# Ternary FFN weights in halves: four cuts and four signs spread over heads 4 to 10 of the first attention

## The chip, the cores and the metric

The kernel runs on one core of a Trainium2 chip. The metric is the device time of one launch in microseconds; lower is better. Each version is run several times and the median counts. A profiled execution also leaves a trace: the start and the duration of every instruction on TensorE (PE, with its weight loads as PEld), VectorE (DVE), ScalarE (ACT), GpSimd (POOL) and the queue engine SyncE (SP), and what ended each idle stretch.

## The reference

The input `x` is 16 samples of 256 tokens by 512. Each sample goes through an attention block that a condition vector modulates, and then through a feed-forward block with ternary weights; the result is added to `x`.

```python
# attention: 16 heads of 32
scale, shift = split(emb @ W_emb + b_emb)
xn = rms_norm(x, g_norm) * (1 + scale) + shift
q, k, v = heads(xn @ W_qkv)
q, k = rms_norm(q, g_q), rms_norm(k, g_k)
o = softmax(q @ k.T * 32 ** -0.5) @ v
y = o + o @ W_out
# feed-forward: 512 -> 2048 -> 512, both weights ternary
def ternarize_weights(w):
    gamma = mean(abs(w))
    return sign(round(w / (gamma + EPS))) * gamma
h = gelu(absmax_quant(layer_norm(y)) @ ternarize_weights(w_fc).T)
out = x + absmax_quant(layer_norm(h)) @ ternarize_weights(w_proj).T
```

Both ternary matrices have 512 x 2048 weights. They are made once, on the chip, while the first samples are already under way.

## The kernel before

The kernel is a pipeline by hand over the 16 samples. `iteration(i)` works on up to five samples at once: it stores sample i-2 (`late`), does the feed-forward block of i-1 (`ffn`), the attention of i (`att`), the q, k, v projections of i+1 (`qkv`) and the input statistics of i+2 (`pre`). Every engine has a program of its own in which these pieces stand in a fixed order; nothing is scheduled at run time. What one engine needs of another it waits for by a semaphore, and an instruction that waits holds back all that stands behind it on its engine.

This case plays in iteration 0, the first attention, which has no feed-forward part. Its loop over the 16 heads is the frame. For head h

- PE computes the scores into a bank of PSUM (L905, `SA` or `SB` by turns, once head 3 is past). It may do so when the bank's scores of two heads before have been read to the end (`plo_r`).
- ACT takes the exponential in place (L1252) and copies it to f16 (`p_hi`, L1258).
- DVE takes the rest, `p_lo` (L1608), which frees the bank.
- PE multiplies with the values, two heads later (`values`, L920 to L922). At the first head of a group of four these products need the shared bank `PV`, which DVE empties with L1457 and L1459 (`heads_out`: `rden`, `o_sb`).

Between the heads stands other work, put at a head by tables. PE computes the q and k of the next sample in four pieces of 512 columns; ACT squares a piece (L1272), DVE sums it (`ssq`, L1634), POOL raises the sums to the power -0.5 (`rqk`, L721), DVE scales the piece (`qkn`, L1638), PE turns it (L1101), ACT and DVE take it apart into f16 pairs (`qkT`, L1294, and L1654 or L1657). The outputs of a group of heads are turned too (L930) and split (`oT_hi` L1327, `oT_lo` L1465). All turns go through one bank `T`, which is free again when DVE has read it (`unturned`).

The ternary weights are made in the same loop. A matrix is held as four parts of 128 x 2048 f32. POOL scales and rounds a part by adding a large constant (L661 for `w_fc`, L691 for `w_proj`). Then the part becomes -1, 0 or 1 in f16, in one of two ways: DVE cuts it off with two instructions, `fc_cut` (L1368 and L1370), or ACT takes the sign with one, `signs` (L1159). `w_fc` parts 2 and 3 go by ACT ahead of the heads, parts 0 and 1 by DVE at heads 4 and 6 (`FC_CUT_AT`). Of `w_proj` ACT does parts 0 and 1 at heads 5 and 6 (`SIGN_AT`), and parts 2 and 3 behind the last head. A sign of `w_proj` writes where a raw part of `w_fc` has lain, so it waits for the cut of that part (`s_fcut`). Who reads the ternary weights comes in iteration 1: `column_sums` on PE (sums of `w_proj`, L767) and `up` (L1005).

Of the kernel before, what the change touches and what calls it, by code (L numbers as in the profile page):

```python
# [16 lines left out]
F = 4 * D  # L17
# [24 lines left out]

HALVES = slice(0, D // 2), slice(D // 2, D)
PIECES = [(0, 0), (0, 1), (1, 0), (1, 1)]

# [56 lines left out]
POOL_PROJ_ROUNDS = (0, 1), (2, 3)  # L102
FC_CUT_AT = {4: 0, 6: 1}
SIGN_AT = {5: (1, 0), 6: (1, 1)}
SIGNS = [(0, 2), (0, 3)] + [SIGN_AT[h] for h in sorted(SIGN_AT)] + [(1, 2), (1, 3)]
WQ_LOW_UNIT, WQ_LOW_AT = {0: (0, 0, KT), 2: (1, 0, KT // 2)}, {1: (1, KT // 2, KT), 2: (2, 0, KT)}
WQ_LOW_DONE = (1, 3, 4)
COLSUM_PART = (0, 1), (1, 2), (2, 4)


# [119 lines left out]
def adaln_ffn_kernel(nc, x, xT, condT, w_emb, b_emb, g_norm, g_qk, w_qkv, w_out, w_fcT, w_projT, out):  # L230
    with ExitStack() as ctx:  # L231
# [274 lines left out]
        def ternary_rows(w, k):  # L506

            return fc_t[:, k, :] if w == 0 else proj_t[:, 4 * k:4 * k + 4, :].rearrange("p k n -> p (k n)")
# [224 lines left out]
        def _(pe):  # L733
# [29 lines left out]
            def column_sums(c):  # L763

                pe.wait_ge(s_sign, SIGNS.index((1, c)) + 1)
                for k in range(4 * c, 4 * c + 4):
                    mm = pe.matmul(FB[0][:, :], ones16[:, :], proj_t[:, k, :], start=(k == 0), stop=(k == FT - 1))  # L767
                if c == 3:
                    mm.then_inc(s_cs, 1)
# [49 lines left out]
            def iteration(i):  # L819
# [221 lines left out]
                for n in range(UNITS):  # L1041
                    if ffn is not None:
                        if n == 0 and not last(ffn):
                            pe.wait_ge(unturned, turn(i, ("y", 1)) + 1)
                        if first(ffn) and n == 0:
                            pe.wait_ge(s_fcut, 2)
                            pe.wait_ge(s_sign, 2)
# [88 lines left out]
        def _(act):  # L1136
# [13 lines left out]

            def signs(w, k):

# [4 lines left out]
                if w:  # L1157
                    act.wait_ge(s_fcut, k // 2 + 1)
                act.activation(ternary_rows(w, k), ffn_raw[w][k], ACT.Sign, bias=unmagic[:, 0:1]).then_inc(s_sign, 1)  # L1159

# [173 lines left out]
        def _(dve):  # L1334
# [26 lines left out]

            def fc_cut(k):

                dst = ternary_rows(0, k)
                if k == 0:
                    dve.wait_ge(wo_h, 2)
                dve.wait_ge(fc_round, POOL_ROUNDS.index(k) + 1)
                dve.tensor_scalar(dst, ffn_raw[0][k], MAGIC, 1.0, ALU.subtract, ALU.min).then_inc(s_cut, 1)  # L1368
                dve.wait_ge(s_cut, k + 1)
                dve.tensor_scalar(dst, dst, -1.0, None, ALU.max).then_inc(s_fcut, 1)  # L1370
# [161 lines left out]
            def iteration(i):  # L1532
# [67 lines left out]
                for h in range(HEADS):  # L1600
# [93 lines left out]
                    if isinstance(i, int) and i == 0 and h in FC_CUT_AT:  # L1694
                        fc_cut(FC_CUT_AT[h])
                    if h == OUT1_AT and ffn is not None:
# [48 lines left out]
```

## Time and profile before

| | us |
|---|---|
| median of 3 runs | 1085.83 |
| lowest, highest | 1084.81, 1086.24 |
| the profiled execution: its time | 1087.22 |
| the same: span from first to last instruction | 1085.2 |
| the same: what lies around the span | 2.0 |
| PE busy, DVE busy, ACT busy, POOL busy | 1051.3, 914.3, 800.6, 559.0 |
| heads of iteration 0, about | 57 to 97 |

The table says which engine has the most to do over the whole span; it does not say what a stretch of 40 us inside it waits for. For that the trace is read by its timeline: each row gives the start, the duration, the engine and the line, and in brackets how long the engine had been idle and which instruction released it.

### The profile page before, as it was taken

What the parts mean: (1) busy time and instruction counts of PE and PEld (TensorE: products, weight loads), DVE (VectorE), ACT (ScalarE), POOL (GpSimd) and SP (SyncE); (2) the same over time, 40 slices, a digit from 0 to 9 for tenths busy, and PEclk for the clock granted to TensorE, in tenths of its full rate; (3) what the DMA queues carried; (4) which work ended last, traced back from release to release, by engine and by line L of the source; (5) the groups of instructions that cost most, each with busy time, mean ns of one, the idle gap of its engine ahead of it and who ended that gap; (6) DMA issues with size and microseconds to landing.
All of it is one profiled execution on the core that took longest, in us unless ns stands there. A gap on an engine that the chain in (4) does not pass through costs nothing. (4 is left out here: it accounts for less than half of the span.)

```text
span 1085.2 us, 24403 instructions
## 1 busy us (share of the span) xinstructions
PE 1051.3 (97%) x9457; PEld 666.1 (61%) x9457; DVE 914.3 (84%) x1629; ACT 800.6 (74%) x1367; POOL 559.0 (52%) x372
## 2 busy tenths in 40 slices
PE   8679999999999999999999999999999999999898
PEld 2334766666576665656666665666656566665666
DVE  4888889888898888989898898989889898868767
ACT  4887877868687785868768586876858688584854
POOL 1953653809356290835629184471917447192613
PEclk9889999999999999999999999999999999999999
DMA  9923112131321313131131312204132220212100
GB/s 343 333 53 73 51 31 74 40 86 58 79 64 23 78 43 79 64 66 61 34 83 45 79 64 55 70 26 93 45 79 65 50 64 32 59 40 60 59 20 21
DMA packets 79698, 77.13 MB, mean 71 GB/s; under 512 B 8656, under 2 KB 60256, under 8 KB 79072
## 3 DMA queue, kind: packets, MB, share of 16 engines
q1 hardware_dynamic: 79552, 75.58, 25.6%
q8 instruction: 75, 1.23, 0.5%
q14 instruction: 39, 0.32, 0.1%
q10 hardware_dynamic: 32, 0.01, 0.0%
HBM read 41.85 MB, written 8.40 MB: 46 GB/s over the span
## 5 line engine op out<-in xcount | busy, mean ns | idle before, releaser
L1005 PE MATMUL F<-yT_hi,fc_t 128*128 128x256 f16 (+1 forms) x1024 | 224.9, 272 | 0.0
L1006 PE MATMUL F<-yT_lo,fc_t 128*128 128x256 f16 (+1 forms) x1024 | 224.6, 272 | 0.0
L721 POOL TENSOR_TENSOR rqk<-ssq,half 128x16 f32<-128x16 f32 x64 | 195.8, 3067 | 36.3 <-DVE ssq L1634 36.3
L843 PE MATMUL F<-proj_t,hs 128*128 128x512 f16 (+1 forms) x512 | 191.7, 376 | 0.0
L845 PE MATMUL F<-proj_t,hs 128*128 128x512 f16 (+1 forms) x512 | 191.3, 375 | 0.0
L1442 DVE SCALAR_TENSOR_TENSOR hs<-hg,g_inv,hs 128x512 f16<-128x512 f32 x128 | 147.7, 1164 | 27.5 <-ACT hs L1309 27.4
L679 POOL TENSOR_TENSOR acc<-acc,hg 128x512 f32<-128x512 f32 x96 | 146.9, 1530 | 14.3 <-ACT hg L1237 1.1
L686 POOL TENSOR_TENSOR acc<-acc,hq 128x512 f32<-128x512 f32 x90 | 114.2, 1269 | 14.2 <-DVE hq L1438 6.0
L1237 ACT ACTIVATE hg<-F,g_fc 128x512 f32<-128x512 f32 x128 | 87.2, 682 | 39.2 <-PE F L1006 38.8
L669 POOL TENSOR_TENSOR rs<-var,half 128x1 f32<-128x1 f32 x32 | 17.7, 552 | 183.8 <-DVE var L1428 183.8
L920 PEld LDWEIGHTS PV<-v_hi,p_hi 128*128 128x128 f16 x1024 | 88.1, 96 | 37.3 <-issue 10.9
L1005 PEld LDWEIGHTS F<-yT_hi,fc_t 128*128 128x128 f16 x1024 | 100.1, 98 | 17.7 <-issue 6.3
L673 POOL TENSOR_TENSOR rx<-msx,half 128x2 f32<-128x2 f32 x16 | 12.4, 776 | 188.9 <-DVE msx L1340 188.9
L920 PE MATMUL PV<-v_hi,p_hi 128*128 128x33 f16 x1024 | 104.5, 178 | 3.6 <-DVE o_sb L1459 2.2
L1006 PEld LDWEIGHTS F<-yT_lo,fc_t 128*128 128x128 f16 x1024 | 100.2, 98 | 11.1
L922 PE MATMUL PV<-v_hi,p_lo 128*128 128x33 f16 x1024 | 103.6, 177 | 0.0
L921 PE MATMUL PV<-v_lo,p_hi 128*128 128x32 f16 x1024 | 103.4, 177 | 0.0
L1608 DVE TENSOR_TENSOR p_lo<-SA,p_hi 128x512 f16<-128x512 f32 x123 | 84.5, 687 | 22.2 <-ACT p_hi L1258 22.1
L921 PEld LDWEIGHTS PV<-v_lo,p_hi 128*128 128x128 f16 x1024 | 83.5, 96 | 23.6 <-issue 0.3
L1608 DVE TENSOR_TENSOR p_lo<-SB,p_hi 128x512 f16<-128x512 f32 x123 | 84.4, 686 | 14.9 <-ACT p_hi L1258 12.1
L1309 ACT ACTIVATE hs<-hg,g_inv 128x512 f16<-128x512 f32 x128 | 92.4, 722 | 5.1
L1252 ACT ACTIVATE SA<-SA 128x512 f32<-128x512 f32 x123 | 72.2, 587 | 14.5 <-PE SA L905 13.7
(265 smaller groups left out, 2756.1 us busy)
## 6 DMA issues: line engine op xcount, KB each, us to landing
stk<-qkT SPq DMA_DIRECT2D x128, 128.0 KB, 2.5
xtok<-in_x SPq DMA_DIRECT2D x17, 512.0 KB, 3.9
xT_sb<-in_xT SPq DMA_DIRECT2D x16, 512.0 KB, 3.5
stk<-qkT SPq DMA_DIRECT2D x128, 64.0 KB, 2.2
xres<-in_x SPq DMA_DIRECT2D x15, 512.0 KB, 3.6
out<-xres SPq DMA_DIRECT2D x15, 512.0 KB, 2.8
stk<-in_w_emb SPq DMA_DIRECT2D x4, 512.0 KB, 6.7
fc_t<-in_w_qkv SPq DMA_DIRECT2D x2, 1024.0 KB, 11.1
```

What stands on the lines that cost most here:

```text
L679: pool.tensor_tensor(acc[:, 0, :], hg[:, 0, :] if n == 1 else acc[:, 0, :], hg[:, n, :], ALU.add).then_inc(sumh_r, 1)
L686: pool.tensor_tensor(acc[:, 1, :], hq[:, 0, :] if n == 1 else acc[:, 1, :], hq[:, n, :], ALU.add).then_inc(sumq_r, 1)
L721: pool.tensor_tensor(rqk[:, n % 2, :], ssq[:, n % 2, :], half[:, :], ALU.pow).then_inc(rqk_r, 1)
L843: pe.matmul(dst, hs[:, 0, k // 2, col:col + P], proj_t[:, k, cols], start=(k == 0), stop=False)
L845: mm = pe.matmul(dst, hs[:, 1, k // 2, col:col + P], proj_t[:, k, cols], start=False, stop=(k == FT - 1))
L920: pe.matmul(dst, ph, v_hi[:, k, h, :], start=(k == 0), stop=False)
L921: pe.matmul(dst[:, 0:DH], ph, v_lo[:, k, h, :], start=False, stop=False)
L922: mm = pe.matmul(dst, p_lo[:, h % (BEHIND + 1), k, t * P:(t + 1) * P], v_hi[:, k, h, :], start=False, stop=(k == TT - 1))
L1005: pe.matmul(dst, w, yT_hi[:, k, cols], start=(k == 0), stop=False)
L1006: mm = pe.matmul(dst, w, yT_lo[:, k, cols], start=False, stop=(k == KT - 1))
L1442: dve.scalar_tensor_tensor(hs[:, 1, n, :], hg[:, n, :], g_inv[:, 0:1], hs[:, 0, n, :], ALU.mult, ALU.subtract).then_inc(hlo_r, 1)
L1608: dve.tensor_tensor(p_lo[:, h % (BEHIND + 1), :, :], score_bank(att, h)[:, :].rearrange("p (k n) -> p k n", k=TT), p_hi[:, h % (BEHIND + 1 ...
```

## The change

The four jobs of the heads loop are cut in half by columns, and the tables place eight halves where four wholes were. `fc_cut(k, part)` does 1024 of the 2048 columns with its two instructions, at heads 4 and 5 (part 0 of `w_fc`), 6 and 8 (part 1). `signs(w, k, part)` does 1024 columns, at heads 6 and 7 (`w_proj` part 0), 9 and 10 (part 1). The semaphores count the halves: a sign of `w_proj` parts 0 and 1 waits for two halves cut, parts 2 and 3 and `up` for four. `signed(w, k)` gives the count of signs after which part k is complete. Nothing of what is computed changes, and PE's and POOL's orders stay as they were.

```diff
+F_HALVES = slice(0, F // 2), slice(F // 2, F)
...
-FC_CUT_AT = {4: 0, 6: 1}
-SIGN_AT = {5: (1, 0), 6: (1, 1)}
+FC_CUT_AT = {4: (0, 0), 5: (0, 1), 6: (1, 0), 8: (1, 1)}
+SIGN_AT = {6: (1, 0, 0), 7: (1, 0, 1), 9: (1, 1, 0), 10: (1, 1, 1)}
...
+def signed(w, k):
+    return max(n for n, sign in enumerate(SIGNS) if sign[:2] == (w, k)) + 1
...
-                pe.wait_ge(s_sign, SIGNS.index((1, c)) + 1)
+                pe.wait_ge(s_sign, signed(1, c))
...
-                            pe.wait_ge(s_fcut, 2)
+                            pe.wait_ge(s_fcut, 4)
...
-            def signs(w, k):
+            def signs(w, k, part=None):
+                cols = slice(0, F) if part is None else F_HALVES[part]
...
-                    act.wait_ge(s_fcut, k // 2 + 1)
-                act.activation(ternary_rows(w, k), ffn_raw[w][k], ACT.Sign, bias=unmagic[:, 0:1]).then_inc(s_sign, 1)
+                    act.wait_ge(s_fcut, 2 * (k // 2 + 1))
+                act.activation(ternary_rows(w, k)[:, cols], ffn_raw[w][k][:, cols], ACT.Sign, bias=unmagic[:, 0:1]).then_inc(s_sign, 1)
...
-            def fc_cut(k):
+            def fc_cut(k, part):
-                dst = ternary_rows(0, k)
-                if k == 0:
+                dst = ternary_rows(0, k)[:, F_HALVES[part]]
+                if k == 0 and part == 0:
                     dve.wait_ge(wo_h, 2)
                 dve.wait_ge(fc_round, POOL_ROUNDS.index(k) + 1)
-                dve.tensor_scalar(dst, ffn_raw[0][k], MAGIC, 1.0, ALU.subtract, ALU.min).then_inc(s_cut, 1)
-                dve.wait_ge(s_cut, k + 1)
+                dve.tensor_scalar(dst, ffn_raw[0][k][:, F_HALVES[part]], MAGIC, 1.0, ALU.subtract, ALU.min).then_inc(s_cut, 1)
+                dve.wait_ge(s_cut, 2 * k + part + 1)
                 dve.tensor_scalar(dst, dst, -1.0, None, ALU.max).then_inc(s_fcut, 1)
```

The first place is DVE at heads 4 to 6. `fc_t<-proj_t` and `fc_t<-fc_t` are the two instructions of a cut, `rden` and `o_sb` empty `PV` for the second group of heads, `p_lo` is the rest of heads 4 (`SA`), 5 (`SB`) and 6 (`SA`). Before:

```order
L1608 TENSOR_TENSOR p_lo<-SA,p_hi 128x512
L1368 TENSOR_SCALAR fc_t<-proj_t 128x2048
L1370 TENSOR_SCALAR fc_t<-fc_t 128x2048
L1457 RECIPROCAL rden<-PV 128x8
L1459 TENSOR_TENSOR o_sb<-PV,rden 128x256
L1608 TENSOR_TENSOR p_lo<-SB,p_hi 128x512
L1634 TENSOR_REDUCE ssq<-sq 128x16
L1638 TENSOR_TENSOR qkn<-QA,rqk 128x512
L1608 TENSOR_TENSOR p_lo<-SA,p_hi 128x512
L1465 TENSOR_TENSOR oT_lo<-T,oT_hi 128x256
L1368 TENSOR_SCALAR fc_t<-proj_t 128x2048
L1370 TENSOR_SCALAR fc_t<-fc_t 128x2048
```

And in the changed kernel, whose lines are numbered seven higher there:

```order
L1615 TENSOR_TENSOR p_lo<-SA,p_hi 128x512
L1375 TENSOR_SCALAR fc_t<-proj_t 128x1024
L1377 TENSOR_SCALAR fc_t<-fc_t 128x1024
L1464 RECIPROCAL rden<-PV 128x8
L1466 TENSOR_TENSOR o_sb<-PV,rden 128x256
L1615 TENSOR_TENSOR p_lo<-SB,p_hi 128x512
L1641 TENSOR_REDUCE ssq<-sq 128x16
L1645 TENSOR_TENSOR qkn<-QA,rqk 128x512
L1375 TENSOR_SCALAR fc_t<-proj_t 128x1024
L1377 TENSOR_SCALAR fc_t<-fc_t 128x1024
L1615 TENSOR_TENSOR p_lo<-SA,p_hi 128x512
L1472 TENSOR_TENSOR oT_lo<-T,oT_hi 128x256
```

The first cut has half the columns, and its second half stands behind `qkn` and ahead of `p_lo` of head 6.

The second place is ACT at heads 5 to 8. `proj_t<-hq` is a sign; `sq<-QB` closes head 5. Before:

```order
L1272 ACTIVATE sq<-QB 128x16x32
L1159 ACTIVATE proj_t<-hq,unmagic 128x2048
L1252 ACTIVATE SA<-SA 128x512
L1258 ACTIVATE p_hi<-SA 128x512
L1327 ACTIVATE oT_hi<-T 128x256
L1159 ACTIVATE proj_t<-hq,unmagic 128x2048
L1252 ACTIVATE SB<-SB 128x512
L1258 ACTIVATE p_hi<-SB 128x512
L1294 ACTIVATE qkT<-T 128x4x128
L1252 ACTIVATE SA<-SA 128x512
L1258 ACTIVATE p_hi<-SA 128x512
```

And in the changed kernel:

```order
L1279 ACTIVATE sq<-QB 128x16x32
L1259 ACTIVATE SA<-SA 128x512
L1265 ACTIVATE p_hi<-SA 128x512
L1334 ACTIVATE oT_hi<-T 128x256
L1166 ACTIVATE proj_t<-hq,unmagic 128x1024
L1259 ACTIVATE SB<-SB 128x512
L1265 ACTIVATE p_hi<-SB 128x512
L1301 ACTIVATE qkT<-T 128x4x128
L1166 ACTIVATE proj_t<-hq,unmagic 128x1024
L1259 ACTIVATE SA<-SA 128x512
L1265 ACTIVATE p_hi<-SA 128x512
```

The sign ahead of head 6 is gone; a half stands behind `oT_hi` of head 6 and another behind `qkT` of head 7.

The third place is ACT at heads 9 to 11. Before:

```order
L1252 ACTIVATE SB<-SB 128x512
L1258 ACTIVATE p_hi<-SB 128x512
L1294 ACTIVATE qkT<-T,g_k 128x4x128
L1252 ACTIVATE SA<-SA 128x512
L1258 ACTIVATE p_hi<-SA 128x512
L1327 ACTIVATE oT_hi<-T 128x256
L1252 ACTIVATE SB<-SB 128x512
```

And in the changed kernel:

```order
L1259 ACTIVATE SB<-SB 128x512
L1265 ACTIVATE p_hi<-SB 128x512
L1301 ACTIVATE qkT<-T,g_k 128x4x128
L1166 ACTIVATE proj_t<-hq,unmagic 128x1024
L1259 ACTIVATE SA<-SA 128x512
L1265 ACTIVATE p_hi<-SA 128x512
L1334 ACTIVATE oT_hi<-T 128x256
L1166 ACTIVATE proj_t<-hq,unmagic 128x1024
L1259 ACTIVATE SB<-SB 128x512
```

Two halves are new here, ahead of the exponentials of heads 10 and 11. On DVE the fourth half of the cuts comes behind the third `ssq`, at head 8.

## Rows read from the trace of the kernel before

**Rows 1.** The page: busy time, share of the span and instructions of each engine.

```profile
PE 1051.3 (97%) x9457; PEld 666.1 (61%) x9457; DVE 914.3 (84%) x1629; ACT 800.6 (74%) x1367; POOL 559.0 (52%) x372
```

**Rows 2.** Windows: stretch and its length, busy time by engine, granted PE clock, DMA.

```profile
57.00:76.50 19.50, 13.01 (x139) 7.27 (x137) 16.78 (x30) 17.06 (x30) 11.36 (x5) 1.00 0.25 62
76.50:83.30 6.80, 6.28 (x30) 3.14 (x31) 5.00 (x10) 4.42 (x9) 2.90 (x1) 0.50 0.01 2
83.30:98.00 14.70, 13.39 (x157) 8.27 (x154) 12.13 (x26) 10.44 (x20) 6.98 (x3) 1.00 0.07 15
200.00:300.00 100.00, 99.95 (x928) 61.97 (x926) 86.48 (x164) 72.86 (x133) 49.63 (x34) 1.00 0.25 60
```

**Rows 3.** Timeline of PE, heads 6 to 12: start, duration, instruction, idle time before.

```profile
70.35 0.18 PE L920 MATMUL PV<-v_hi,p_hi 128*128 128x33 f16 x1 [1.52 <-DVE o_sb L1459]
...
74.19 0.63 PE L1101 MATMUL T<-ident,qkn 128*128 128x128 f32 x4 [1.31 <-DVE oT_lo L1465]
...
77.03 0.61 PE L905 MATMUL SB<-stk 97*128 97x256 f16 x2 [1.69 <-DVE p_lo L1608]
...
80.55 1.09 PE L1101 MATMUL T<-ident,qkn 128*128 128x128 f32 x4
...
86.13 0.39 PE L773 MATMUL QA<-wq_hi,xn_hi 128*128 128x512 f16 x1 [0.79 <-DVE qkn L1638]
```

**Rows 4.** Timeline of DVE, heads 4 to 7.

```profile
67.01 1.90 DVE L1368 TENSOR_SCALAR fc_t<-proj_t 128x2048 f16<-128x2048 f32 x1
68.94 0.69 DVE L1370 TENSOR_SCALAR fc_t<-fc_t 128x2048 f16<-128x2048 f16 x1
...
70.12 0.68 DVE L1608 TENSOR_TENSOR p_lo<-SB,p_hi 128x512 f16<-128x512 f32 x1
...
72.43 0.69 DVE L1638 TENSOR_TENSOR qkn<-QA,rqk 128x512 f32<-128x512 f32 x1 [1.01 <-POOL rqk L721]
73.03 0.68 DVE L1608 TENSOR_TENSOR p_lo<-SA,p_hi 128x512 f16<-128x512 f32 x1
...
73.96 1.22 DVE L1368 TENSOR_SCALAR fc_t<-proj_t 128x2048 f16<-128x2048 f32 x1
...
76.28 0.69 DVE L1608 TENSOR_TENSOR p_lo<-SB,p_hi 128x512 f16<-128x512 f32 x1 [0.37 <-ACT p_hi L1258]
```

**Rows 5.** Timeline of POOL, 39 to 91 us; a row with x2 merges two instructions.

```profile
39.34 0.69 POOL L673 TENSOR_TENSOR rx<-msx,half 128x2 f32<-128x2 f32 x1
...
63.90 3.93 POOL L691 TENSOR_SCALAR hq<-hq,inv 128x2048 f32<-128x2048 f32 x2 [8.65 <-DVE wo_lo L1379]
67.79 1.88 POOL L673 TENSOR_TENSOR rx<-msx,half 128x2 f32<-128x2 f32 x1
69.46 5.80 POOL L721 TENSOR_TENSOR rqk<-ssq,half 128x16 f32<-128x16 f32 x2
...
87.61 3.07 POOL L721 TENSOR_TENSOR rqk<-ssq,half 128x16 f32<-128x16 f32 x1 [5.26 <-DVE ssq L1634]
```

**Rows 6.** Timeline of ACT, heads 5 to 12.

```profile
67.28 0.59 ACT L1272 ACTIVATE sq<-QB 128x512 f32<-128x512 f32 x1
69.73 2.00 ACT L1159 ACTIVATE proj_t<-hq,unmagic 128x2048 f16<-128x2048 f32 x1 [1.86 <-DVE fc_t L1370]
71.64 0.58 ACT L1252 ACTIVATE SA<-SA 128x512 f32<-128x512 f32 x1
72.31 0.60 ACT L1258 ACTIVATE p_hi<-SA 128x512 f16<-128x512 f32 x1
...
81.68 0.69 ACT L1294 ACTIVATE qkT<-T,g_k 128x512 f16<-128x512 f32 x1 [2.10 <-PE T L1101]
...
84.64 0.38 ACT L1327 ACTIVATE oT_hi<-T 128x256 f16<-128x256 f32 x1 [1.09 <-PE T L930]
84.92 0.59 ACT L1252 ACTIVATE SB<-SB 128x512 f32<-128x512 f32 x1
...
88.42 0.60 ACT L1294 ACTIVATE qkT<-T 128x512 f16<-128x512 f32 x1 [0.55 <-PE T L1101]
```

More of the change, by code:

```diff
@@ L1694, in iteration @@
                     if isinstance(i, int) and i == 0 and h in FC_CUT_AT:
-                        fc_cut(FC_CUT_AT[h])
+                        fc_cut(*FC_CUT_AT[h])
                     if h == OUT1_AT and ffn is not None:
```

## Prediction

> **What bounds the kernel now.** I read the busy line first [rows 1]: PE is busy 97% of the span. Then I compared stretches [rows 2]: from 200 to 300 us PE is busy 99.95 of 100 us, so there only PE's own work counts and anything gained or lost earlier is carried to the end unchanged. From 57 to 76.5 us, where the change lies, PE is busy only 13.01 of 19.50 us, and no engine is full (DVE 16.78, ACT 17.06). This stretch is bound by waits between in-order engines. From 76.5 to 83.3 us PE's granted clock is 0.50, the lower level of 1.2 GHz, and before and behind it 1.00.
>
> Third, the timeline of PE for what ended its waits. Three stand before the clock falls [rows 3]: 1.52 us for `o_sb`, 1.31 us for `oT_lo`, 1.69 us for `p_lo` of head 7. Each is followed back in the other timelines:
> - `o_sb` stands behind the first cut on DVE, which starts at 67.01 and ends at 69.63 (68.94 + 0.69) [rows 4].
> - `oT_lo` stands behind `p_lo` of head 6, and that behind `qkn`, which waited 1.01 us for POOL's power until 72.43 [rows 4].
> - `p_lo` of head 7 waited for ACT, where two signs of 2.00 us stand around head 6, the first after 1.86 us of waiting for the cut [rows 4, 6].
>
> So the whole-sized jobs do lie on the path. The question is where the halves come to lie.
>
> **What a half costs.** `L1368` took 1.22 us at 73.96 and 1.90 at 67.01 [rows 4]. The longer one began while POOL's L691 ran, which ended at 67.83 (63.90 + 3.93) [rows 5]; I read the 0.68 us between as DVE waiting for POOL. A half should then cost 0.61 us and the second instruction 0.35 (half of 0.69), 0.95 for a pair against 1.90 without the wait. Per-instruction overhead is not halved, so the truth is at or slightly above this; a half can't cost more than the whole. The sign: half of 2.00 plus a little, 1.05 us, with 0.1 of it beside its neighbour, as 69.73 + 2.00 overlaps 71.64 [rows 6]. Work added by the splitting: two DVE pairs and two ACT instructions more, by overhead alone some 0.1 us each.
>
> **Part by part, head by head.**
> 1. First half cut, head 4. It ends at 67.01 + 0.68 + 0.95 = 68.65 instead of 69.63, a gain of 0.9 to 1.0. If the 0.68 halves as well, the gain is 1.3; if nothing but the elements counts less, 0.8. I take 0.9, nearest the clean 1.22 row. `o_sb`, `p_lo` of head 5, PE's products at 70.35 and its scores of head 7 come 0.9 earlier.
> 2. The sign ahead of head 6 is gone. ACT is free after `sq` at 67.87 [rows 6], so the exponential of head 6 starts at about 67.8 instead of 71.64. This looks like 3.8 us, but it is spent at once: what reads it, `p_lo` of head 6, stands on DVE behind `qkn` and now behind a half cut.
> 3. POOL's `rx` took 1.88 us, 0.69 when alone, and ended with DVE's cut (67.79 + 1.88 = 69.67) [rows 5]. The power for `qkn` follows it. With the cut over 0.9 earlier, the power ends at 71.5, `qkn` starts at 71.5 instead of 72.43, the half cut takes 72.1 to 73.05, and `p_lo` of head 6 starts at 73.05: before 73.03 [rows 4]. The gain is exactly eaten. Bounds: if POOL doesn't start earlier, it is 0.9 later; if the cut costs less, 0.1 earlier. `oT_lo`, and PE's turn at 74.19 behind it, stay where they were.
> 4. ACT's first half sign waits for that second half cut: 73.15 to 74.2. Then the exponential and copy of head 7 (steps of 0.68 and 0.60, as in rows 6) end at 75.4, and `p_lo` of head 7 starts at 75.5 instead of 76.28, after the third half cut, which fits ahead of it from 74.0 to 74.95. PE's scores of head 9 start at 76.25 instead of 77.03: a gain of 0.8.
> 5. The second half sign, behind `qkT` at 75.35 to 75.9, ends at 76.9; the exponential of head 8 starts at 76.8, before 76.6 (0.2 later).
> 6. PE's pieces and the turn at 80.55 come 0.75 earlier, 79.8, since PE is at half clock in both. ACT's `qkT` comes at 80.95 instead of 81.68. Before, ACT had idled 2.10 us there [rows 6], but now the third half sign follows, 81.5 to 82.5, and the exponential of head 10 starts at 82.5 instead of 82.3.
> 7. PE reaches the turn for `oT_hi` 0.4 earlier (the clock comes back at 83.3 in either kernel, so work done before that point is worth half): `oT_hi` 84.25 instead of 84.64. The fourth half sign stands behind it, 84.5 to 85.5, so the exponential of head 11 starts at 85.45 instead of 84.92: 0.5 later.
> 8. What is late next: ACT idled 0.55 us before `qkT` at 88.42 [rows 6] and takes up that 0.5. PE's wait of 0.79 at 86.13 for `qkn` ends up to 0.4 earlier. The `ssq` that starts POOL's last power, 87.61 + 3.07 = 90.68 [rows 5], comes 0.5 later, and its reader began at 90.8; so 0.4 late there, mostly behind PE work, since PE is busy 13.39 of 14.70 us in that stretch [rows 2]. I keep 0 to +0.25.
>
> Sum: -0.9 at head 6, 0 at head 6's rest, -0.8 at head 9, +0.5 at head 11, absorbed at head 12: between -0.4 and +0.3 at the end of the heads, and I take -0.1. Behind it are four half waits that don't bind: `column_sums` and `up` need the halves at 101 us and later, all are done by 86. The profiled execution would go from 1087.22 (span 1085.2 + 2.0) to 1087.1; its time lies 1.4 above the median shown, and applied to the median 1085.83 the forecast is 1085.7.
>
> **The rivals.**
> *A, the clock stays up.* The fall at 76.5 follows a stretch in which PE waited 1.31 and 1.69 us with little between [rows 3]. Of this the second wait shrinks to 0.9, but the first grows: PE arrives 0.9 earlier at a turn that stays at 74.19, so 2.2 us. The total is the same 3.1, so I expect the fall to come again. For the rival: it lies otherwise in time, and after 75.5 PE is better fed. If it doesn't fall, the turn comes at 78.5 instead of 79.8, DVE's `o_sb` and ACT's half signs decide, and the exponential of head 11 starts at 83.8 instead of 84.92: -1.1, time 1084.7.
>
> *B, the second half cut is late.* If POOL's power isn't moved by the shorter cut, `qkn` stays at 72.43 and the half cut pushes `p_lo` of head 6 and the first half sign 0.9 back. Then every step from 3 on is 0.9 later; the idle of ACT before its turns (2.10, 1.09, 0.55) takes up part of it. Price +0.3 to +0.9, time 1086.4. It decides as soon as the power ends later than 71.5. For it: one POOL row only shows the coupling. Against it: that `rx` ended within 0.05 us of the cut.
>
> *C, a cut is shut out by POOL's power.* The second half cut starts at 72.1, when POOL works on its second power, 71.5 to 74.4 (2.90 each, rows 5). If DVE had to wait for the power's end, the pair would end at 75.3, `p_lo` of head 6 start 2.2 later and PE's turn with it; after the idle of ACT is used up, +1.6 remain, time 1087.4, slower than before. It decides from 71.5 on, whenever a power runs at the cut's start. Against it stands the cut at 73.96: the power ran until 75.26 (69.46 + 5.80), and `L1368` took its plain 1.22 us [rows 4, 5].
>
> The Trainium skill, "SBUF — State Buffer", section on what the engines share, makes rival C a rule: a VectorE `tensor_scalar` in a two-port mode and a GpSimd instruction exclude each other for the whole instruction, and the later one fully blocks. By that rule the sum would be 1087.4. The trace agrees for L691 against L1368 (0.68 us lost) and for `rx` (1.88 against 0.69), and disagrees for the power; the measurement decides, so C gets a small chance.
>
> **How the numbers follow.** My forecast has 0.56, A 0.24, B 0.13, C 0.04; 0.03 is for what I haven't seen. What a measurement of this kernel can tell from no change is 0.2%, 2.2 us. The forecast and B lie well inside it, A reaches it only with another microsecond from the scatter of the runs (1084.81 to 1086.24), C for about one case in three. So faster 0.05, same 0.91, slower 0.04. The range runs from A with 0.5 us of scatter below, 1084.2, to B's far end, 1086.7, with 0.3 above: 1087.0.
>
> **What would show it.** Right: the half `L1368` at head 4 at about 1.3 us and the others at 0.6; `p_lo` of head 6 within 0.2 of where it was relative to the scores of head 4; ACT waiting over 2 us for the second half cut; the exponential of head 9 earlier and that of head 11 later. A: a clock row without 0.50 between 70 and 85. B: `qkn` at 72.4. C: an `L1368` of 128x1024 that takes over 1.5 us beside a power. The forecast is wrong if the first matmul of iteration 1's `up` moves by more than 1 us.

## The result, and the profile after

The changed kernel is slower: median 1087.88 us (1086.51 to 1089.57, 22 runs) against 1086.16 us (1084.58 to 1088.20, 22 runs) of the kernel before on the same chip, a ratio of 1.0016 with a 95% interval of 1.0010 to 1.0022. Forecast were 1085.7 us, a range of 1084.2 to 1087.0, and no change, with 0.91. The ratio lies inside the 0.2% that the prediction took for its limit of no change, but its interval leaves out 1.0000, and the median lies above the range; 0.33 us of the distance is the kernel before, whose median had been 1085.83 in the 3 runs shown ahead. The profiled execution took 1088.09 us, with a span of 1086.2 us. In two of the experiments below one run took 3.7 ms, and the ratios leave it out.

The busy line of the page of the changed kernel (engine, busy us, share, instructions) answers to [rows 1]:

```profile
PE 1053.2 (97%) x9457; PEld 665.6 (61%) x9457; DVE 915.1 (84%) x1633; ACT 800.5 (74%) x1369; POOL 559.0 (51%) x372
```

Four instructions more on DVE and two on ACT cost 0.8 us and nothing in busy time. PE's busy time rose by 1.9 us at the same 9457 instructions; the same instruction lasts longer at the lower clock (the scores of head 9 below 0.61 us, 0.39 at the full clock). So no engine has gained work that would account for the loss; where the time goes has to be read stretch by stretch. The windows of the changed kernel, with the columns of [rows 2]:

```profile
57.00:76.50 19.50, 14.42 (x141) 7.80 (x139) 16.29 (x32) 14.57 (x29) 11.29 (x5) 0.93 0.26 62
76.50:83.30 6.80, 6.02 (x45) 3.08 (x46) 5.92 (x12) 6.03 (x10) 3.04 (x1) 0.75 0.01 2
83.30:98.00 14.70, 12.51 (x141) 7.76 (x141) 11.98 (x26) 11.65 (x22) 7.22 (x4) 1.00 0.07 14
200.00:300.00 100.00, 99.93 (x921) 61.95 (x920) 86.64 (x164) 72.74 (x131) 50.14 (x34) 1.00 0.25 60
```

The second row reads 0.75 where [rows 2] have 0.50: this execution had 3.4 us of the lower clock in the heads, and the profiled one of before had 6.8 (added up over windows of 1 us). The 0.93 of the first row is the end of an earlier stretch of low clock, which lasted until 56.0 us in the trace of before and until 59.8 here. It cost nothing in the heads: the exponential of head 5 comes 7.53 to 7.55 us after that of head 0 in every trace of this document, in one of which that stretch lasted until 63.2 (signs alone, filled). ACT now has 2.5 us less work ahead of 76.5 (14.57 against 17.06) and 1.6 more from 76.5 to 83.3: the signs have moved there.

DVE at heads 4 to 8 of the changed kernel answers to [rows 4]:

```profile
67.14 1.35 DVE L1375 TENSOR_SCALAR fc_t<-proj_t 128x1024 f16<-128x1024 f32 x1
68.53 0.43 DVE L1377 TENSOR_SCALAR fc_t<-fc_t 128x1024 f16<-128x1024 f16 x1
...
69.44 0.68 DVE L1615 TENSOR_TENSOR p_lo<-SB,p_hi 128x512 f16<-128x512 f32 x1
...
71.98 0.69 DVE L1645 TENSOR_TENSOR qkn<-QA,rqk 128x512 f32<-128x512 f32 x1 [1.25 <-POOL rqk L727]
72.59 0.68 DVE L1375 TENSOR_SCALAR fc_t<-proj_t 128x1024 f16<-128x1024 f32 x1
73.31 0.43 DVE L1377 TENSOR_SCALAR fc_t<-fc_t 128x1024 f16<-128x1024 f16 x1
73.65 0.68 DVE L1615 TENSOR_TENSOR p_lo<-SA,p_hi 128x512 f16<-128x512 f32 x1
...
78.89 0.69 DVE L1615 TENSOR_TENSOR p_lo<-SA,p_hi 128x512 f16<-128x512 f32 x1 [0.81 <-ACT p_hi L1265]
```

PE and POOL there, to [rows 3] and [rows 5]:

```profile
74.81 0.63 PE L1107 MATMUL T<-ident,qkn 128*128 128x128 f32 x4 [2.61 <-DVE oT_lo L1472]
...
76.93 0.61 PE L911 MATMUL SB<-stk 97*128 97x256 f16 x2 [0.98 <-DVE p_lo L1615]
```

```profile
67.91 1.16 POOL L679 TENSOR_TENSOR rx<-msx,half 128x2 f32<-128x2 f32 x1
69.05 6.27 POOL L727 TENSOR_TENSOR rqk<-ssq,half 128x16 f32<-128x16 f32 x2
80.27 3.28 POOL L727 TENSOR_TENSOR rqk<-ssq,half 128x16 f32<-128x16 f32 x1 [4.95 <-DVE ssq L1641]
```

And ACT at heads 6 to 11, to [rows 6]:

```profile
67.89 0.60 ACT L1259 ACTIVATE SA<-SA 128x512 f32<-128x512 f32 x1
...
73.83 1.15 ACT L1166 ACTIVATE proj_t<-hq,unmagic 128x1024 f16<-128x1024 f32 x1 [3.02 <-DVE fc_t L1377]
74.89 0.57 ACT L1259 ACTIVATE SB<-SB 128x512 f32<-128x512 f32 x1
...
81.69 1.14 ACT L1166 ACTIVATE proj_t<-hq,unmagic 128x1024 f16<-128x1024 f32 x1
82.73 0.59 ACT L1259 ACTIVATE SA<-SA 128x512 f32<-128x512 f32 x1
...
84.17 1.15 ACT L1166 ACTIVATE proj_t<-hq,unmagic 128x1024 f16<-128x1024 f32 x1
85.21 0.60 ACT L1259 ACTIVATE SB<-SB 128x512 f32<-128x512 f32 x1
```

The last two half signs start with no idle time ahead of them and hold up the exponentials of heads 10 and 11 by 1.04 us each (81.69 to 82.73, 84.17 to 85.21). Before, ACT had idled 2.10 and 1.09 us there ahead of `qkT` and `oT_hi` [rows 6].

**How the two profiled executions differ.** I cut both at three points: the exponential of head 0, the first `bn` of iteration 1 (end of the heads), and DVE's write of `mrow` in iteration 1, from where PE is full.

| stretch, us | before | changed | difference |
|---|---|---|---|
| start to exponential of head 0 | 58.56 | 58.69 | +0.13 |
| to the first `bn` of iteration 1 | 41.39 | 41.34 | -0.05 |
| to `mrow` of iteration 1 | 21.65 | 21.64 | -0.01 |
| to the end | 963.61 | 964.50 | +0.89 |

At first sight the heads are innocent. That reading is false, since the two had unlike clocks, and the 0.89 is a second matter.

### The profile page after: what moved, and what is told of

It is laid out like the page before. It is cut to its first block and busy times, and to the rows that moved or that the text cites. A ratio compares the mean times of both kernels' runs of the same rounds, so it can differ in the third digit from the quotient of the medians.

```text
span 1086.2 us, 24411 instructions
## 1 busy us (share of the span) xinstructions
PE 1053.2 (97%) x9457; PEld 665.6 (61%) x9457; DVE 915.1 (84%) x1633; ACT 800.5 (74%) x1369; POOL 559.0 (51%) x372
```

## The experiments

Each kernel ran 11 times, the kernel before beside it 27 or 33 times on the same chip (medians 1086.03 to 1086.31), and a ratio compares these two. "Heads", "low clock" and "rest" are those of the one profiled execution. "Heads" is the second row of the table above, "rest" the last; "low clock" is how long TensorE was granted 1.2 GHz in the heads from 66 us on. The expectations below take the end of a trace to 0.1 us, so their rests are up to 0.05 us off (963.96 for 964.01 or 963.92).

| kernel | median | ratio to before, 95% | heads | low clock | rest |
|---|---|---|---|---|---|
| before again | 1086.40 | 1.0002 (0.9993 to 1.0011) | 41.32 | 6.8 | 963.56 |
| changed again | 1087.42 | 1.0011 (1.0003 to 1.0020) | 41.82 | 6.8 | 963.92 |
| before, filled | 1084.64 | 0.9985 (0.9977 to 0.9994) | 39.01 | 0 | 963.55 |
| changed, filled | 1087.97 | 1.0014 (1.0005 to 1.0023) | 41.10 | 0 | 964.34 |
| cuts alone | 1087.63 | 1.0014 (1.0005 to 1.0023) | 41.42 | 6.8 | 963.86 |
| signs alone | 1086.44 | 1.0004 (0.9995 to 1.0013) | 41.35 | 3.4 | 963.51 |
| cuts alone, filled | 1086.77 | 1.0008 (0.9999 to 1.0017) | 42.03 | 3.4 | 963.89 |
| signs alone, filled | 1085.24 | 0.9995 (0.9986 to 1.0004) | 39.81 | 0 | 963.55 |
| split in place | 1087.05 | 1.0013 (1.0004 to 1.0021) | 41.14 | 6.8 | 963.93 |
| before, four memsets | 1086.61 | 1.0001 (0.9992 to 1.0010) | 40.28 | 3.4 | 963.95 |
| gap | 1085.86 | 0.9998 (0.9989 to 1.0007) | 39.55 | 3.4 | 963.95 |
| gap, filled | 1084.65 | 0.9988 (0.9979 to 0.9997) | 38.24 | 0 | 964.01 |
| single wait | 1087.53 | 1.0012 (1.0003 to 1.0021) | 41.08 | 3.4 | 963.99 |
| changed, twelve memsets | 1087.71 | 1.0014 (1.0005 to 1.0023) | 41.70 | 6.8 | 963.71 |
| gap, filled, twelve memsets | 1084.52 | 0.9984 (0.9975 to 0.9992) | 38.25 | 0 | 963.88 |

**The two kernels again.** No edit.

> The kernel before, unchanged, as a control: ratio 1.000. It also gives a second trace and the granted clock of each run. Clock theory (the change makes TensorE's clock fall in the first attention more often, or for longer, than before): most of its runs spend less time at the lower clock than the trace shown before, whose stretch at 0.50 lasted 6.8 us, and have a higher mean clock than those of the changed kernel. Order theory (the half signs ahead of the exponentials of heads 10 and 11 hold ACT back, whatever the clock does): no difference in mean clock. Landing theory (loads land by chance, the two medians differ by which loads PE meets): the point at which iteration 1 starts is the same in both kernels and the difference arises behind 108 us.

> The changed kernel, unchanged: ratio 1.001 to 1.002 as measured. Clock theory: lower mean clock than before_again by the stretch that it loses, some 3 us at half clock (0.0015 of the mean). Order theory: same mean clock, first up-projection matmul about 1.5 us later than in before_again. Landing theory: first up-projection matmul at the same time as in before_again, within 0.3 us.

The loss is there again, somewhat smaller. This trace of the changed kernel had 6.8 us of low clock as that of before has, and its heads are 0.46 us longer (41.82 against 41.36, the mean of 41.39 and 41.32). So some loss is there at an equal clock. The clock theory isn't ruled out beside it: the granted clock of whole runs is 0.9910 on average in these 11 and 0.9902 in the 22 of the result, against 0.9919 in the 11 of before again and 0.9909 to 0.9916 in the runs of before beside the experiments. A difference of 0.001 is some 2.2 us more at half clock, and a mean doesn't say whether they lie in the heads or ahead of them, where they cost nothing.

**Filling TensorE's waits.** Small products on a free bank (`keep_busy`) stand in the waits of heads 6 to 9, so that the clock stays up. The edit is the same in all filled kernels, with other counts:

```diff
+BUSY_SCORES, BUSY_VALUES, BUSY_TURN = {9: 4}, {6: 2}, {7: 10}
...
+                                keep_busy(FB[0], BUSY_SCORES.get(h, 0))
```

> The changed kernel with dummy matmuls of TensorE into a free bank in its three waits: 2 ahead of the values of head 4, 10 ahead of the turn at head 7, 4 ahead of the scores of head 9 (0.22 us each, so they fit into waits of 0.7, 2.6 and 1.0 us). Clock theory: the clock stays up, and the kernel gains 1 to 2 us, ratio 0.999 to 1.000. Order theory: ACT and DVE decide, so it stays at 1.0016. Landing theory: it stays at 1.0016.

> The kernel before with dummy matmuls of TensorE into a free bank in its three waits: 5 ahead of the values of head 4, 5 ahead of the turn at head 7, 6 ahead of the scores of head 9 (waits of 1.5, 1.3 and 1.7 us). Clock theory: if before rarely falls, no gain, ratio 1.000; if it falls as in its trace, up to 1.5 us faster, ratio 0.9985. Order theory and landing theory: at most 0.5 us faster.

The kernel before gains 0.15% from a clock that stays up, the changed one gains nothing. Exponential of head 11, counted from that of head 0: 26.36 to 23.70 us in the kernel before, 26.52 to only 26.29 in the changed one. The small products themselves hold nothing up: the exponential of head 9 comes at 20.53 in the changed kernel and 19.72 in that before, within 0.02 of where it came without them. ACT of the filled kernel before, heads 9 to 11:

```profile
80.16 0.69 ACT L1300 ACTIVATE qkT<-T,g_k 128x512 f16<-128x512 f32 x1 [0.33 <-PE T L1107]
80.75 0.59 ACT L1258 ACTIVATE SA<-SA 128x512 f32<-128x512 f32 x1
...
82.23 0.38 ACT L1333 ACTIVATE oT_hi<-T 128x256 f16<-128x256 f32 x1 [0.21 <-PE T L931]
82.51 0.59 ACT L1258 ACTIVATE SB<-SB 128x512 f32<-128x512 f32 x1
```

And the same stretch of the filled changed kernel:

```profile
81.13 0.68 ACT L1307 ACTIVATE qkT<-T,g_k 128x512 f16<-128x512 f32 x1
81.70 1.15 ACT L1172 ACTIVATE proj_t<-hq,unmagic 128x1024 f16<-128x1024 f32 x1
82.74 0.60 ACT L1265 ACTIVATE SA<-SA 128x512 f32<-128x512 f32 x1
...
84.38 0.38 ACT L1340 ACTIVATE oT_hi<-T 128x256 f16<-128x256 f32 x1 [0.36 <-PE T L937]
84.66 1.14 ACT L1172 ACTIVATE proj_t<-hq,unmagic 128x1024 f16<-128x1024 f32 x1
85.70 0.59 ACT L1265 ACTIVATE SB<-SB 128x512 f32<-128x512 f32 x1
```

With a fast TensorE, ACT's idle of 2.10 us [rows 6] has shrunk to 0.33 in the first listing: there is no room for a half sign any more. In the second, two of them stand in ACT's nearly full row (0.36 us idle). So at an equal clock the change costs in the heads: 0.46 us with 6.8 us of low clock, 1.06 with 3.4 (41.34 against 40.28, the kernel before with four memsets, below), 2.09 with none (41.10 against 39.01).

**Half of the change at a time.** Cuts alone keeps the whole signs at heads 5 and 6, signs alone the whole cuts at 4 and 6:

```diff
-SIGN_AT = {6: (1, 0, 0), 7: (1, 0, 1), 9: (1, 1, 0), 10: (1, 1, 1)}
+SIGN_AT = {5: (1, 0), 6: (1, 1)}
```

> Only the cuts are halved and spread as in the change; the signs stay whole, at heads 5 and 6, and wait for the half whose place they write (1 half and 2 halves). Sign theory (a half sign that stands behind head 7, 9 or 10 lies on ACT's path once TensorE runs at full clock, some 1 us each): the cuts cost little, ratio 0.999 to 1.0005. Cut theory (the second half cut ahead of the p_lo of head 6 pushes p_lo, turn and scores back): it carries the loss of the change, ratio 1.001 to 1.002.

> Only the signs are halved and spread as in the change (heads 6, 7, 9, 10); the cuts stay whole at heads 4 and 6. Sign theory: it carries the loss of the change, ratio 1.0005 to 1.002. Cut theory: ratio 0.999 to 1.000, since ACT is free for the exponential of head 6 at once.

> As cuts_only, with dummy matmuls in TensorE's waits (2 ahead of the values of head 4, 10 ahead of the turn at head 7, 7 ahead of the scores of head 9), so that the clock stays up. Sign theory: within 0.6 us of before_busy, ratio 0.998 to 0.999. Cut theory: as slow as after_busy, 1.001 or more.

> As signs_only, with dummy matmuls in TensorE's waits (5 ahead of the values of head 4, 5 ahead of the turn at head 7, 5 ahead of the scores of head 9), so that the clock stays up. Sign theory: the exponential of head 11 comes 1.5 to 2.5 us later after that of head 0 than the 23.7 us of before_busy, ratio 1.000. Cut theory: within 0.5 us of before_busy, ratio 0.9985.

Each part costs by itself once PE is fast. Signs alone at 3.4 us of low clock takes 41.35 us in the heads against 40.28, and with the clock up 39.81 against 39.01. Cuts alone at 6.8 us takes 41.42 against 41.36, next to nothing; its median (1.0014) is more than that and the 0.3 us of its rest account for, and its runs had a lower clock on average (0.9897 against 0.9916). Its fill didn't keep the clock up to the end, but the clock fell only at 85.0 us, behind the exponential of head 12, so up to there the filled traces can be compared. That exponential comes 25.36 us after that of head 0 in the kernel before, 26.87 with the cuts alone (+1.51), 26.66 with the signs alone (+1.30), 27.95 with both (+2.59). By the end of the heads the 1.30 have shrunk to 0.80 and the 2.59 to 2.09.

The cuts' cost arises at two places. The first is the second half cut ahead of `p_lo` of head 6: in every trace of a kernel that has it, that `p_lo` starts 14.96 us after the exponential of head 0, against 14.47 before. In cuts alone the whole sign at head 6 waits for this cut as well, and the exponential of head 7 starts at 17.05 instead of 16.40. The second is the fourth half cut, at head 8. DVE of cuts alone, filled, and below it of the filled kernel before:

```profile
79.70 0.69 DVE L1381 TENSOR_SCALAR fc_t<-proj_t 128x1024 f16<-128x1024 f32 x1
80.42 0.43 DVE L1383 TENSOR_SCALAR fc_t<-fc_t 128x1024 f16<-128x1024 f16 x1
80.76 0.20 DVE L1470 RECIPROCAL rden<-PV 128x8 f32<-128x8 f32 x1
...
81.34 0.68 DVE L1621 TENSOR_TENSOR p_lo<-SB,p_hi 128x512 f16<-128x512 f32 x1
81.93 0.74 DVE L1667 SCALAR_TENSOR_TENSOR qkT<-T,g_k,qkT 128x512 f16<-128x512 f32 x1
```

```profile
79.68 0.21 DVE L1463 RECIPROCAL rden<-PV 128x8 f32<-128x8 f32 x1
...
80.26 0.68 DVE L1614 TENSOR_TENSOR p_lo<-SB,p_hi 128x512 f16<-128x512 f32 x1
80.88 0.75 DVE L1660 SCALAR_TENSOR_TENSOR qkT<-T,g_k,qkT 128x512 f16<-128x512 f32 x1
```

DVE has no idle time here, so the half cut takes 1.06 us from what stands behind it. `p_lo` of head 9 comes 1.55 later (23.00 against 21.45), though its exponential came only 0.64 later, and `qkT` frees the bank `T` late. PE's turn for `oT_hi` waits for that:

```profile
82.82 0.41 PE L937 MATMUL T<-ident,o_sb 128*128 128x128 f32 x2 [0.72 <-DVE qkT L1667]
```

ACT then idles 1.08 us, and the exponential of head 11 is 1.50 late, where that of head 10 was 0.64 late. The filled changed kernel has the same wait of PE for `qkT`, 0.80 us.

**Split in place.** All halves back to back where the wholes stood:

```diff
-FC_CUT_AT = {4: (0, 0), 5: (0, 1), 6: (1, 0), 8: (1, 1)}
-SIGN_AT = {6: (1, 0, 0), 7: (1, 0, 1), 9: (1, 1, 0), 10: (1, 1, 1)}
+FC_CUT_AT = {4: ((0, 0), (0, 1)), 6: ((1, 0), (1, 1))}
+SIGN_AT = {5: ((1, 0, 0), (1, 0, 1)), 6: ((1, 1, 0), (1, 1, 1))}
```

> The changed kernel with all halves at the heads where the wholes were: both cut halves of a part back to back at heads 4 and 6, the sign halves back to back at heads 5 and 6. It prices the splitting itself: a pair of halves of a cut takes 2 x 1.12 us less overlap where a whole took 1.9, a sign 2 x 1.05 where it took 1.9. Order theory: +0.2 to +0.6 us on the heads and 0.44 from the place of DVE's instructions, ratio 1.0005 to 1.001. If the splitting alone is the loss, 1.0014.

The heads come out as before (41.14 against 41.32 and 41.39 at the same clock), and still it is 0.13% slower. Part of that lies behind the heads, 0.3 to 0.4 us (963.93 against 963.56 and 963.61), and its cause comes next. The other 0.9 us or so no single pair of traces shows. What fits is the clock: this trace lies at the median of its kernel, while the two of before with 6.8 us lie 0.6 and 1.4 us above theirs, and the granted clock of all its runs is 0.9896 on average against 0.9909. Against the heads of before at 3.4 us of low clock (40.28, below) its 41.14 are 0.86 more. Why its clock should be low for longer isn't shown.

**Four memsets.** The kernel before, with four writes of 128x1 on DVE ahead of everything, as many DVE instructions as the change adds:

```diff
+            for k in range(4):
+                dve.memset(pad[:, k:k + 1], 0.0).then_inc(pad_r, 1)
```

> The kernel before with four DVE memsets of 128x1 into a tile that nothing reads, at the very start, where DVE waits anyway. They count as many instructions as the change adds to DVE. Place theory (in the traces of every kernel with more cuts, and in none without, DVE idles 0.46 us instead of 0.10 ahead of bn_aggr at 356 us and loses some 0.1 us at two more places and 0.1 to 0.2 near the end; this goes with how far DVE's instruction stream is shifted, not with what the instructions do): from the maxima row of iteration 1 to the end it takes 963.96 us instead of 963.52, ratio 1.0004. Rival (the gaps come from the changed work): 963.52, ratio 1.000.

The rest becomes 963.95 us instead of 963.51 to 963.61, by 0.34 to 0.44. So the mere shift of DVE's instructions has this price: the five traces without more DVE instructions (before, again and filled, signs alone and filled) lie at 963.51 to 963.61, those with four more at 963.86 and above. DVE of before at the start of iteration 5:

```profile
355.19 0.70 DVE L1423 BATCH_NORM_STATS2 bn<-SA 128x6 f32<-128x512 f32 x1
355.99 0.18 DVE L1426 BATCH_NORM_AGGREGATE mv<-bn 128x2 f32<-128x6 f32 x1
```

And of before with four memsets:

```profile
354.13 0.70 DVE L1427 BATCH_NORM_STATS2 bn<-SA 128x6 f32<-128x512 f32 x1
355.28 0.18 DVE L1430 BATCH_NORM_AGGREGATE mv<-bn 128x2 f32<-128x6 f32 x1 [0.46 <-DVE bn L1427]
```

The same pair of instructions, 0.80 us apart in the one and 1.15 in the other, and the second waits for nothing but the first in both. The changed kernel has the same stall (355.74 and 356.89). The timed median of the kernel with four memsets shows no clear loss (1.0001), which means that the 0.4 us is below what one such comparison can tell.

**Twelve memsets.** The same loop with 12 in place of 4, ahead of the changed kernel and, further below, of the best one.

> The changed kernel with 12 small VectorE memsets ahead of everything, so that its instruction stream lies elsewhere. Theory that 0.44 us of the loss hangs on the place of VectorE's instructions: the time from the write of mrow in iteration 1 to the end, 963.5 in the kernel before and 963.9 with four instructions more, is neither by chance again but moves by 0.2 or more to either side, and the ratio with it by 0.0002 or more, the memsets' own cost (under 1 us at the start, beside the loads) aside. Rival, the 0.44 us come from the count of instructions in the heads and not from their place: 963.9 again and 1.0011 to 1.0017.

The stall moved but did not go. DVE's write of `mrow`, once per iteration (63.80 us apart as a rule):

```profile
504.89 0.41 DVE L1592 TENSOR_SCALAR mrow<-T 16x256 f16<-16x256 f32 x1
...
568.85 0.41 DVE L1592 TENSOR_SCALAR mrow<-T 16x256 f16<-16x256 f32 x1
...
632.64 0.41 DVE L1592 TENSOR_SCALAR mrow<-T 16x256 f16<-16x256 f32 x1
```

Here one iteration takes 63.96 us (504.89 to 568.85), and those that took 63.88 and 63.90 in the changed kernel take 63.80. The rest is 963.71, 0.21 and 0.28 below the 963.92 and 963.99 of the changed kernel again and the one with the single wait: just what I had asked for, and the moved iteration decides for place and against count. By how much the place can lower the price stays open: the gap kernel with twelve, below, kept nearly all of it. Its heads had 6.8 us of low clock, and the median shows no gain.

**A single wait.** The half signs of the first part of `w_proj` wait only for the first half cut, which frees the place that they overwrite. Cuts alone and the gap kernels have the same line:

```diff
-                    act.wait_ge(s_fcut, 2 * (k // 2 + 1))
+                    act.wait_ge(s_fcut, k + 1 if k < 2 else 4)
```

> The changed kernel in which a half sign of the first projection part waits only for the half cut that it overwrites (one half), and not for the pair (two halves). Path theory: ScalarE's half sign at head 6, which waited 3.02 us for the second half of the first cut, starts some 2.5 to 3 us earlier, and exp(7) with it; the half signs behind heads 7, 9 and 10 cost on, so the heads are longer than those of the kernel before at an equal clock by 0.3 to 1 us, and the ratio is 1.0005 to 1.0012. Rival, the half signs' place alone costs and the wait was free: 1.0016 as the changed kernel.

ACT then has no wait of 3.02 us. The sign starts in the gap behind `oT_hi`, and the exponential of head 7 follows 13.08 us after that of head 0 instead of 16.20:

```profile
70.90 0.38 ACT L1334 ACTIVATE oT_hi<-T 128x256 f16<-128x256 f32 x1 [1.26 <-PE T L936]
71.18 1.14 ACT L1166 ACTIVATE proj_t<-hq,unmagic 128x1024 f16<-128x1024 f32 x1
75.95 0.60 ACT L1301 ACTIVATE qkT<-T 128x512 f16<-128x512 f32 x1 [2.46 <-PE T L1107]
```

Yet ACT then idles 2.46 us for PE's turn, which stands behind the late `oT_lo`. The heads fall by 0.26 us (41.34 to 41.08, both at 3.4 us of low clock), and 0.80 of 1.06 stay. So the strictest wait of the change, 3.02 us long, holds a quarter of its cost in the heads, by one trace of each.

**The gap.** DVE waits 1.25 us for POOL's power ahead of `qkn` of head 5. I placed the second half cut in that wait, both halves of the second cut at head 6, and the signs whole as before:

```diff
-FC_CUT_AT = {4: (0, 0), 5: (0, 1), 6: (1, 0), 8: (1, 1)}
-SIGN_AT = {6: (1, 0, 0), 7: (1, 0, 1), 9: (1, 1, 0), 10: (1, 1, 1)}
+FC_CUT_AT, FC_CUT_EARLY = {4: ((0, 0),), 6: ((1, 0), (1, 1))}, {5: (0, 1)}
+SIGN_AT = {5: (1, 0), 6: (1, 1)}
...
+                    if isinstance(i, int) and i == 0 and h in FC_CUT_EARLY:
+                        fc_cut(*FC_CUT_EARLY[h])
```

> The cuts halved, the second half of w_fc part 0 placed between ssq and qkn of head 5, where DVE idles 1.0 us for POOL's power; both halves of part 1 at head 6; the signs whole at heads 5 and 6, each waiting for the half whose place it writes. Sign and cut theory together (a half costs only where its engine is full): exponential of head 6 1.3 us earlier than before, p_lo of head 6 0.4 to 0.6 earlier, scores of head 9 up to 0.9 earlier; with the clock falling as before the end of the heads moves by 0 to -0.5. Ratio 0.999 to 1.0005 (0.44 us of it the place of DVE's instructions). If the cut ahead of qkn delays POOL or qkn, 1.001.

> As gap, with dummy matmuls in TensorE's waits (2 ahead of the values of head 4, 6 ahead of the turn at head 7, 4 ahead of the scores of head 9). With the clock up throughout: start of the heads to the first bn_stats 38 to 38.7 us, where before_busy took 39.0; ratio 0.998 to 0.9985. If the waits are now too short for the dummies or the clock falls elsewhere, 0.9985 to 1.000.

> The variant with the first half cut before the normalisation of head 5, whole signs, and 12 additional small products that keep TensorE occupied (it measured 0.9988), with 12 small VectorE memsets ahead of everything. Place theory: the stretch from mrow of iteration 1 to the end differs from its 963.96 by 0.2 or more, and where it falls to 963.5 the ratio is 0.9980 to 0.9986. Rival: 963.96 and 0.9988 again.

DVE of the filled gap kernel, heads 5 and 6:

```profile
71.01 0.68 DVE L1381 TENSOR_SCALAR fc_t<-proj_t 128x1024 f16<-128x1024 f32 x1
71.72 0.43 DVE L1383 TENSOR_SCALAR fc_t<-fc_t 128x1024 f16<-128x1024 f16 x1
72.34 0.69 DVE L1653 TENSOR_TENSOR qkn<-QA,rqk 128x512 f32<-128x512 f32 x1 [0.18 <-POOL rqk L728]
72.94 0.68 DVE L1621 TENSOR_TENSOR p_lo<-SA,p_hi 128x512 f16<-128x512 f32 x1
```

The wait for POOL is filled with the cut (0.18 left of 1.25), `qkn` is not late, and `p_lo` of head 6 starts 13.89 us after the exponential of head 0, 1.07 earlier than in the changed kernel and 0.58 earlier than before. The heads take 0.73 us less than before at 3.4 us of low clock and 0.77 less with none. With the fill this version beats both unfilled kernels: 0.9988 and, with the twelve memsets, 0.9984 (0.9975 to 0.9992) against before. With the twelve memsets the stall moved again (one iteration of 64.08 us, none of 63.88 or 63.90), and the rest is 963.88 against 964.01, less than the 0.2 that the place theory asked for. The gap alone gives 0.9998: its 0.7 us less the 0.4 of the shifted instructions is too little to be told from nothing. The fill on the kernel before alone gives 0.9985, so most of the gain is the clock's, and how much of it the gap holds beside the fill these medians can't tell.

## Why the prediction was wrong

Measured from the exponential of head 0, step by step:

1. *First half cut, `o_sb` and `p_lo` of head 5 0.9 earlier.* Held: `p_lo` of head 5 came 0.81 earlier (10.75 against 11.56). The half cut took 1.35 us beside L691, as asked, and the pairs elsewhere 0.68 and 0.43.
2. *The exponential of head 6 3.8 us earlier.* Held: 3.88 (9.20 against 13.08).
3. *The gain is exactly eaten at `p_lo` of head 6.* This step failed first; its price for a half pair and its time for the power were both off. POOL's power let `qkn` start 0.58 earlier, not 0.93, though `rx` fell from 1.88 to 1.16 as I had read. And a half pair holds DVE for 1.06 us (72.59 to 73.65), not 0.95. So `p_lo` of head 6, `oT_lo` and PE's turn came 0.49 later, not at the same time.
4. *The exponential and `p_lo` of head 7 0.8 earlier.* 0.20 and 0.22. The half sign started at 73.83 behind the late cut and took 1.15 with a step of 1.06, where I had 1.05 with a step of 0.95.
5. *The exponential of head 8 0.2 later.* 0.81 later (18.87 against 18.06), by the sum of steps 3 and 4 and of the second half sign. From here on the changed kernel is behind. The sum then leaves out a term: the fourth half cut, at head 8, has no step of its own. It stands in DVE's full row from 80.10 to 81.17, ahead of `rden`, `o_sb`, `p_lo` of head 9 and `qkT`. In cuts alone, filled, it took the delay from 0.64 at the exponential of head 10 to 1.50 at that of head 11.
6. *The exponential of head 10 0.2 later.* 0.33 later in numbers, but with 3.4 us less of low clock. At an equal clock it is 1.18 (24.04 against 22.86).
7. *That of head 11 0.5 later.* 0.16 in numbers, 1.27 at an equal clock (26.52 against 25.25).
8. *Absorbed at head 12, so -0.1 at the end of the heads.* The two profiled executions differ by -0.05, which looks like a hit and is not one: at an equal clock the end is 0.46, 1.06 or 2.09 later. Little absorbs it, since ACT has little idle time in heads 9 to 12 once PE is fast: 1.27 at head 11 has become 1.06 at the end at 3.4 us of low clock, and 2.59 has become 2.09 with none.

**The common error** is the one ahead of all steps: every stretch was compared with one profiled execution of before, which had 6.8 us of low clock and lay 1.4 us above the median of its kernel. In it ACT idles 2.10 and 1.09 us for a slow PE, and there half signs look free. In executions with less low clock that cover is mostly gone (0.33 and 0.21 us in the filled kernel before). The trace with four memsets (3.4 us) has the heads 1.04 us shorter than before again, at the same instructions from head 0 on.

**Rival A** (the clock stays up, 1084.7) had the condition partly right and the sign wrong. The low clock was shorter in the profiled run of after, and kept away in the filled one. But a clock that stays up gives the changed kernel 0.23 us at head 11 and not 1.1, while it gives the kernel before 2.66: I had let DVE's `o_sb` and ACT decide at 83.8 and not counted the two half signs in ACT's row, nor the fourth half cut in DVE's. **Rival B** named the right place (the second half cut ahead of `p_lo` of head 6) and, with +0.3 to +0.9, nearly the right price, 0.49 there. Its condition was half met: the power ended 0.58 us earlier, which is between its 0 and the 0.93 of the forecast, and the other 0.1 came from the dearer half pair. **Rival C** fell: the half cut that started at 72.59 while POOL's power ran took 0.68 us, as one of 0.69 at 74.58 did. The Trainium skill, "SBUF — State Buffer", section "Who interferes with whom", would have DVE blocked there for the whole power; the trace disagrees again. What the rows do show is the reverse: the power took 3.28 us beside the fourth half cut against 2.90 in the kernel before, and the pair of powers 6.27 against 5.80. In the pair the power ends 0.05 us behind the end of a cut's first instruction (75.32 against 74.58 + 0.69 = 75.27; 75.67 against 75.62 in the filled gap kernel).

**The rest of the kernel** I had taken as unchanged ("carried to the end unchanged", from [rows 2]). It holds two things. One is the 0.4 us of the shifted DVE instructions, which no step had. The other shows in two of the five traces of the changed kernel and its two variants (single wait, twelve memsets), the profiled run of the result and the filled one: ACT waited for the load of `xtok` in iteration 1. Of the first:

```profile
172.28 0.63 ACT L1184 ACTIVATE junk<-xtok 128x512 bf16<-128x512 f32 x1 [1.89 <-DMA xtok<-in_x]
```

and of the filled changed kernel:

```profile
172.49 0.63 ACT L1190 ACTIVATE junk<-xtok 128x512 bf16<-128x512 f32 x1 [1.60 <-DMA xtok<-in_x]
```

In before that row starts at 171.41 after 1.07 us. The interval from the `mrow` of iteration 1 to the next is 64.04 us instead of 63.55, by 0.49; the stalls make up the other 0.40 of 0.89. In the filled one it is 63.76. The other three (the changed kernel again, the single wait, the twelve memsets) have 63.52 to 63.54, so I count it to the single execution; whether the change makes it more frequent stays open.

**The sum that fits.** 0.46 to 2.09 us in the heads at an equal clock, and 0.4 behind them: 0.9 to 2.5 us. Measured were 0.16% (1.7 us, interval 1.1 to 2.4) and 0.11% (1.2 us, 0.3 to 2.2). What stays open: how often each length of low clock comes in the heads, since the other runs give only a mean over the whole span; how much of the loss is a clock that is low for longer in the changed kernel, as the means of whole runs suggest (0.9902 and 0.9910, though its own heads change by no more than 0.72 us with the clock, 41.10 to 41.82); how the 2.09 divides, since cuts and signs by themselves add up to more than both together (1.51 and 1.30 against 2.59); and what makes DVE stall at a shifted place.

## What to carry to other kernels

A wait in one trace may be the work of a slow clock in that execution. Before you put work into an engine's idle time, ask whether that time is still there when the engine that it waits for runs at full speed; where the profiled execution lies above the median, assume that it is not. Put a split piece into a wait that another engine's fixed work sets, as POOL's power here, and not behind the instruction that ends the wait. And a longest wait is not a largest cost: 3.02 us taken away were worth 0.26.

## What the runs showed of the hardware

- The place of instructions costs time. Four small DVE instructions ahead of everything made stalls of up to 0.46 us far behind, in iterations 5 and 10 and in the tail, 0.34 to 0.44 us in all; with twelve they stood elsewhere.
- The changed kernel ran its heads with 3.4 us at 1.2 GHz in one execution and 6.8 in another (41.34 and 41.82 us); the kernel before with 6.8, and with four small instructions ahead of it 3.4. Small products in PE's waits kept the granted clock at 1.00 from 66 us to the end of the heads in five of six filled kernels, worth 2.3 us in the heads of the kernel before (41.32 to 39.01).
- A half of an instruction costs more than half: 0.43 against 0.69 (f16 to f16) and 1.15 against 2.00 (the sign), 0.68 against 1.22 (the cut).
- GpSimd's power slowed from 2.90 to 3.28 us beside a half cut on DVE, and DVE did not. In the changed and the filled gap kernel the slowed power ended 0.05 us behind the cut's first instruction (f32 to f16), which points at that one; no run takes the two apart.
